# Second attention: the causal mask of a head added by sixteen 32x32 products instead of four 128x128 ones

## The chip, the cores and the metric

The kernel runs on one core of one Trainium2 chip. The metric is device microseconds from start to end of one execution; lower is better. A core has a matrix engine (PE), whose weight loads the profile shows apart (PEld), a vector engine (DVE), an activation engine (ACT), a general engine (POOL) and a queue that issues transfers (SP). PE writes its results to eight PSUM banks, which DVE and ACT read.

## What is computed

A transformer of four layers over x with 16 sequences of 256 tokens and 128 features. The layers are an attention with 2 heads, a feed-forward part, a second attention with 16 heads of 8 features and a causal mask, and the same feed-forward part again. The second attention is what matters here:

```python
qkv = encodings @ attn_w.T + attn_b
q, k, v = jnp.split(qkv, 3, axis=-1)          # 16 heads, 8 features each
mask = jnp.arange(n)[:, None] <= jnp.arange(n)[None, :]
scores = jnp.einsum('bhki,bhqi->bhkq', k, q) / math.sqrt(HEAD)
scores = jnp.where(mask, scores, NEG_INF)
probs = jax.nn.softmax(scores, axis=2)        # over the keys
combined = jnp.einsum('bhkq,bhkl->bhql', probs, v)
out = out @ out_w.T + out_b
```

## The kernel before

The 16 sequences are worked in 8 blocks of 2 sequences (512 tokens), block 0 to block 7, and each layer runs over the 8 blocks before the next layer begins, with some overlap at the seams. Every engine has its own program in a fixed order, written out by hand; semaphores tie them together. Blocks 1 to 6 run in a loop or in copies of its body.

In the second attention a block has 8 steps (n = 0 to 7), each for one group of 4 heads and one sequence. Scores are made twice. `pe_first` makes them queries by keys for the block after the current one, so that DVE (`dve_first`, two reductions b_segment_max at L1599) can take each query's maximum. `pe_second` makes them keys by queries for the current block, with the maximum already in the operands, and ACT (`act_exp`, b_prob at L1504) takes the exponential. POOL zeroes the masked part of the probabilities (L1709), and `pe_values` multiplies them with v.

The four heads of a group lie in four groups of 32 rows of the operands, `rows_of(j)`. A product over 32 rows occupies a quarter of the array's rows, so four heads' products can run side by side. In the trace they are the matmuls with shape 32*128 of f_h_lo and f_h_hi (these tiles hold q and k in this layer); head j writes PSUM bank j of first_pass. The values' products have shape 128*16: all rows, 16 columns of weights. The mask is added inside the same accumulation: for each head a product of the identity ident_b with the tile mask (0, or -1e30 above the diagonal), shape 128*128 with 256 moving columns, both bf16.

One step on PE is, in this order: pe_second for heads 0 and 1, pe_first with its mask products, pe_second for heads 2 and 3, pe_values of the step before, and in most steps a piece of other work (transposes, projections of a later block, the output projection). What PE waits for:

- pe_first waits for DVE's reductions of the step before, since there is one set of first_pass banks; in steps 0 and 4 also for the rows that a transfer brings.
- each pe_second waits for ACT's exponential of the pair before, since there is one pair of second_pass banks.
- pe_second's second half stands behind the mask products in PE's queue.

The firsts of block 0 are made earlier, one after each chunk of the last feed-forward block of the layer ahead (`pe_front`, block LAST = 7 there). I call this the front.

Transfers are issued by SP in order (`sp_out`, then `sp_rows`): the weighted values of the block before go to DRAM (b_o_dram), come back as oT and den, the inverse of den goes out and back, and only then are q and k of the block two ahead stored and loaded again in their row layout. `sp_out` begins when ACT has copied the last group's values in step 0.

The mask and the identity are made by POOL near the start of the program (`pool_b_constants`, L272 to L281). The first attention, which runs before that layer, has its own POOL work in each block: rstd (L207), X plus bias (L774), the rotated keys a_kT and queries a_qT (L766), and the low parts of weights, wlo (L851). DVE there waits for most of these, and scales a_prob (L666) and normalises xn (L182) from SBUF to SBUF.

In the last block of the second attention no firsts are made; two products of ident_b with 512 columns of mask per step fill PE there.

Of the kernel before, what the change touches and what calls it, by code (L numbers as in the profile page):

```python
# [18 lines left out]
BF16 = mybir.dt.bfloat16  # L19
# [66 lines left out]
def build(nc, io):  # L86
    ctx = ExitStack()
    with ctx:
# [166 lines left out]
        ident_b = sb("b_ident", [P, P], BF16)  # L255
        mask = sb("b_mask", [P, GROUPS, P], BF16)

# [13 lines left out]
        def pool_b_constants(pool):  # L271
            nc.gpsimd.memset(constant_rows[:, :, :], 0.0).then_inc(s_cr, 1)  # L272
            nc.gpsimd.memset(ident_b[:, :], 0.0).then_inc(s_cp, 1)
            nc.gpsimd.memset(mask[:, :, :], 0.0).then_inc(s_cp, 1)
            pool.wait_ge(s_cr, 1)
            nc.gpsimd.memset(constant_rows[0:1, 1, :], 1.0).then_inc(s_cr, 1)

            pool.wait_ge(s_cp, 2)
            nc.gpsimd.affine_select(out=ident_b[:, :], in_=ident_b[:, :], compare_op=ALU.not_equal, fill=1.0,
                                    base=0, pattern=[[-1, P]], channel_multiplier=1).then_inc(s_cp, 1)  # L280
            nc.gpsimd.affine_select(out=mask[:, 0:3:2, :], in_=mask[:, 0:3:2, :], compare_op=ALU.is_ge, fill=MASKED,  # L281
                                    base=0, pattern=[[0, 2], [-1, P]], channel_multiplier=1).then_inc(s_cp, 1)

# [9 lines left out]
        def attention_a(link):  # L293
# [475 lines left out]
            def pool_body(pool, b, before, one, two):  # L769
# [5 lines left out]
                if one:  # L775
                    pool_rope(pool, b.after(1), 1)
                if two and not is_block(b, 0):
                    ffn["beside"]["pool"](pool, b.after(2))
# [414 lines left out]
        def attention_b(link):  # L1193
# [97 lines left out]
            def pe_first(pe, m, n):  # L1291
# [7 lines left out]
                for qt, into in ((1, slice(P, 3 * P)), (0, slice(0, P))):  # L1299
                    for j in range(GROUPS):  # L1300
                        mm(first_pass[:, j, into], q[rows_of(j), g, at + qt * P:at + (qt + 1) * P],
                           k[rows_of(j), g, at:at + (qt + 1) * P], start=qt == 1, stop=False)
                for j in range(GROUPS):
                    out = first_pass[:, j, 0:3 * P].rearrange("p (c k) -> p c k", c=3)
                    last = mm(out[:, 0:3:2, :], ident_b[:, :], mask[:, 0:3:2, :], start=False, stop=True)
                last.then_inc(s_p1, 1)
# [65 lines left out]
            def pe_step(pe, b, n, before, one, two, parts=None):  # L1372
# [15 lines left out]
                if not one and n > 2:  # L1388
                    if n == 3:
                        pe.wait_ge(nxt["split_written"], 1)  # L1390
                    for _ in range(2):
                        mm(misc[:, :], ident_b[:, :], mask[:, :, :].rearrange("p g k -> p (g k)"))
                if n:
# [588 lines left out]
```

## Time and profile before

| | |
|---|---|
| runs of the kernel (us) | 740.25, 737.65, 735.57; median 737.65 |
| span of the profiled execution | 729.4 us |
| own time of the profiled execution | not recorded beside the span; the median lies 8.25 us above the span |
| instructions in the profile | 13978 |
| busy: PE / DVE / ACT / POOL | 665.8 / 497.1 / 451.8 / 425.8 us |
| mean granted clock of PE | 0.990 |
| first attention, feed-forward, front | 0 to 124, 124 to 303, 303 to 328 us |
| second attention, second feed-forward | 328 to about 545, then to the end |

The busy times say how much work an engine has, not who is waited for. The time is a chain of work from start to end; an instruction made shorter gives time back only where it lies on that chain, and only until something else is late.

### The profile page before, as it was taken

The page shows a single profiled execution, that of the slowest core. Times are in us where ns is not written, and L with a number is a line of the kernel's source. Part 1 is how long each engine was busy: PE and PEld are TensorE (multiplying, and loading weights), DVE is VectorE, ACT ScalarE, POOL GpSimd, SP SyncE. Part 2 cuts the span into 40 slices and gives each one's busy share as a digit, 9 for nine tenths or more (in the row PEclk, how much of TensorE's full clock was granted, in tenths as well). Part 3 has the DMA queues.
Part 4 walks back from the last instruction along what each step waited for, and adds up shares of the span by engine and source line. Part 5 has one row for each costly group of instructions (what it writes and reads, how often), then busy time and mean ns, then how long its engine had stood idle before and what let it go on. Part 6 is the DMA issues. An engine that isn't in the chain of part 4 may idle for free.

```text
span 729.4 us, 13978 instructions
## 1 busy us (share of the span) xinstructions
PE 665.8 (91%) x4716; PEld 467.1 (64%) x4716; DVE 497.1 (68%) x958; ACT 451.8 (62%) x801; POOL 425.8 (58%) x443
## 2 busy tenths in 40 slices
PE   3889997799999999998999999998988999999997
PEld 1455654478777776675555655655546777877785
DVE  6769998577656688456867867865668667776521
ACT  2668887456666666445666666665675566566664
POOL 4545543277877777434444554543565777777773
PEclk9989999999999999999999999999999999999999
DMA  6101230000000001730645754745122000000000
GB/s 191 40 21 41 57 37 1 1 1 1 1 0 0 1 0 45 245 116 29 229 144 184 260 165 169 249 148 182 38 69 92 0 15 15 14 0 15 16 14 30
DMA packets 33028, 52.47 MB, mean 72 GB/s; under 512 B 4560, under 2 KB 9680, under 8 KB 32976
## 3 DMA queue, kind: packets, MB, share of 16 engines
q1 hardware_dynamic: 32784, 51.53, 22.4%
q8 instruction: 30, 0.49, 0.3%
q10 hardware_dynamic: 192, 0.26, 0.1%
q14 instruction: 22, 0.18, 0.1%
HBM read 27.15 MB, written 24.38 MB: 71 GB/s over the span
## 4 chain that ended last, share of the span: by engine, by line
PE 57%; DVE 18%; issue 8%; ACT 7%; DMA 6%; POOL 2%; SPq 1%; DVEq 1%; ACTq 0%; POOLq 0%
PE banks L220 54%; DVE b_segment_max L1599 3%; ACT b_prob L1504 3%; DVE xn L182 3%; DMA b_o_dram<-b_o 3%; DVE a_mx L652 2%; DMA f_h_lo<-b_k_dram 1%; ACT a_prob L553 1%; DMA b_den<-b_o_dram 1%; DVE f_gate L1088 1%; DVE f_h_hi L1091 1%; PE banks L212 1%; PE banks L977 1%; DVE f_hidden L1094 1%; DVE a_prob L666 1%
## 5 line engine op out<-in xcount | busy, mean ns | idle before, releaser
L1158 POOL TENSOR_TENSOR f_g_lo<-f_gelu,f_g_hi 128x512 fp32r<-128x512 f32 x127 | 162.9, 1292 | 53.5 <-ACT f_g_hi L1044 53.0
L1043 ACT ACTIVATE f_gelu<-banks,cols 128x512 f32<-128x512 f32 x128 | 88.3, 690 | 130.6 <-PE banks L220 108.7
L1709 POOL TENSOR_SCALAR_AFFINE_SELECT b_prob<-b_prob 128x512 f32<-128x512 f32 x128 | 81.5, 638 | 107.0 <-ACT b_prob L1504 106.5
L1599 DVE TENSOR_REDUCE b_segment_max<-banks 128x6 f32<-128x768 f32 x128 | 116.1, 949 | 33.4 <-PE banks L220 33.2
L1504 ACT ACTIVATE b_prob<-banks 128x768 f32<-128x768 f32 x128 | 102.3, 806 | 55.7 <-PE banks L220 55.7
L220 PE MATMUL banks<-f_g_hi,whi 128*128 128x512 f32 x320 | 130.4, 408 | 1.9 <-POOL f_g_lo L1158 1.4
L220 PE MATMUL banks<-f_g_lo,whi 128*128 128x512 f32 x320 | 126.7, 396 | 0.0
L1151 POOL TENSOR_TENSOR f_h_lo<-f_hidden,f_h_hi 128x512 fp32r<-128x512 f32 x60 | 77.6, 1293 | 62.8 <-DVE f_hidden L1094 61.1
L220 PE MATMUL banks<-f_h_hi,whi 128*128 128x512 f32 x256 | 104.3, 407 | 6.1 <-POOL f_h_lo L1151 3.3
L220 PE MATMUL banks<-f_h_lo,whi 128*128 128x512 f32 x256 | 101.5, 396 | 0.0
L1044 ACT ACTIVATE f_g_hi<-banks,cols 128x512 fp32r<-128x512 f32 x128 | 87.4, 682 | 0.0
L1088 DVE SCALAR_TENSOR_TENSOR f_gate<-f_tanh,banks 128x512 f32<-128x512 f32 x64 | 43.3, 677 | 53.3 <-ACT f_tanh L1035 53.3
L220 PE MATMUL banks<-f_xn_split,whi 128*128 128x512 f32 x256 | 71.6, 402 | 1.3 <-DVE f_hidden L1094 1.3
L182 DVE TENSOR_SCALAR xn<-X,mv,rstd 128x128 f32<-128x128 f32 (+1 forms) x104 | 72.3, 760 | 0.4 <-POOL rstd L207 0.4
L220 PEld LDWEIGHTS banks<-f_g_hi,whi 128*128 128x128 f32 x320 | 60.3, 188 | 17.6 <-POOL f_g_lo L1158 3.5
L220 PEld LDWEIGHTS banks<-f_g_lo,whi 128*128 128x128 f32 x320 | 60.4, 189 | 13.2 <-issue 0.2
L220 PEld LDWEIGHTS banks<-f_h_hi,f_h_lo 32*128 32x128 f32 x512 | 37.0, 184 | 45.7 <-ACT b_prob L1504 23.6
L220 PE MATMUL banks<-f_h_hi,f_h_lo 32*128 32x128 f32 (+1 forms) x512 | 54.9, 300 | 10.8 <-ACT b_prob L1504 7.2
L220 PEld LDWEIGHTS banks<-f_h_hi,whi 128*128 128x128 f32 x256 | 48.2, 188 | 22.8 <-POOL f_h_lo L1151 4.4
L220 PE MATMUL banks<-b_prob,b_values 128*16 128x256 f32 (+1 forms) x1024 | 56.1, 332 | 2.2 <-POOL b_prob L1709 1.5
L220 PEld LDWEIGHTS banks<-f_xn_split,whi 128*128 128x128 f32 x256 | 48.1, 190 | 15.1 <-DVE f_hidden L1094 2.0
L220 PEld LDWEIGHTS banks<-f_h_lo,whi 128*128 128x128 f32 x256 | 48.2, 188 | 11.1 <-issue 0.5
(125 smaller groups left out, 1061.0 us busy)
## 6 DMA issues: line engine op xcount, KB each, us to landing
f_h_hi<-b_q_dram SPq DMA_DIRECT2D x16, 512.0 KB, 4.0
f_h_lo<-b_k_dram SPq DMA_DIRECT2D x16, 512.0 KB, 5.0
b_o_dram<-b_o SPq DMA_DIRECT2D x8, 1024.0 KB, 4.3
b_q_dram<-b_q_hi SPq DMA_DIRECT2D x16, 256.0 KB, 3.3
b_k_dram<-b_k_hi SPq DMA_DIRECT2D x16, 256.0 KB, 3.6
w_stage<-in_wF SPq DMA_DIRECT2D x8, 352.0 KB, 3.2
b_q_dram<-b_q_lo SPq DMA_DIRECT2D x8, 256.0 KB, 3.4
b_k_dram<-b_k_lo SPq DMA_DIRECT2D x8, 256.0 KB, 3.7
```

Of the source, the lines that this page charges most:

```text
L182: nc.vector.tensor_scalar(xn[:, s, :], X[:, bass.ds(TILES * t + s, 1), :], mv[:, s, 0:1], rstd[:, s:s + 1], ALU.subtract, ALU.mult).then_i ...
L212: last = nc.tensor.transpose(bank[:, s * P:(s + 1) * P], xn[:, s, :], ident[:, :])
L220: return nc.tensor.matmul(out, lhsT, rhs, start=start, stop=stop)
L652: nc.vector.reduce_max(mx[s][:, :, :], score[:, :, :].rearrange("p h (q k) -> p h q k", q=2), AX.X).then_inc(s_mx, 1)
L1043: nc.scalar.activation(gf[c % 2][:, :], z_bank[c % 2], ACT.Gelu, scale=scale).then_inc(s_gf, 1)
L1044: nc.scalar.activation(hi[:, c, :], z_bank[c % 2], ACT.Gelu, scale=scale).then_inc(s_ghi[c % 2], 1)
L1088: nc.vector.scalar_tensor_tensor(out=uu[slot][:, :], in0=th[slot][:, :], scalar=1.0, in1=a[:, :], op0=ALU.add, op1=ALU.mult).then_inc(s_u, 1)
L1151: nc.gpsimd.tensor_tensor(hlo[n.odd][:, c, :], hf[c % 2][:, :], hhi[n.odd][:, c, :].bitcast(F32), ALU.subtract).then_inc(s_hlo[c % 2], 1)
L1158: nc.gpsimd.tensor_tensor(lo[:, c, :], gf[c % 2][:, :], hi[:, c, :].bitcast(F32), ALU.subtract).then_inc(s_glo[c % 2], 1)
L1504: nc.scalar.activation(prob[n % 2][:, p, :, :, :], second_banks(b, p)[:, :, 0:3 * P].rearrange("p b (c q) -> p c b q", c=3), ACT.Exp, scal ...
L1599: nc.vector.reduce_max(seg[:, g, s, 2 * p:2 * p + 2, :], first_pass[:, 2 * p:2 * p + 2, 0:3 * P].rearrange("p b (c k) -> p b c k", c=3), A ...
L1709: nc.gpsimd.affine_select(out=pr, in_=pr, compare_op=ALU.is_ge, fill=0.0, base=0, pattern=[[0, 4], [1, P]], channel_multiplier=-1).then_in ...
```

## The change

For each head j and each group i of 32 queries, the mask is now added by a product of 32 rows (the identity's rows and columns of `rows_of(j)`, shape 32*32) with 256 moving columns from the mask's rows `rows_of(j)`. Four such products make up what was one, so a step has 16 mask products instead of 4. The products of one head use that head's row group only; the 16 products of a step name 16 different 32x32 parts of the array. For this the mask tile grows from 4 x 128 to 7 x 2 x 128 columns: one diagonal position for each difference of i and j. Its zeroing and its filling move on POOL from the start of the program into blocks 5 and 6 of the first attention, and are 1792 columns wide instead of 512 and 256. The fillers of the last block read the first 512 columns of the new tile.

```diff
-        mask = sb("b_mask", [P, GROUPS, P], BF16)
+        mask = sb("b_mask", [P, 2 * GROUPS - 1, 2, P], BF16)
...
-            nc.gpsimd.memset(mask[:, :, :], 0.0).then_inc(s_cp, 1)
...
-            nc.gpsimd.affine_select(out=mask[:, 0:3:2, :], in_=mask[:, 0:3:2, :], compare_op=ALU.is_ge, fill=MASKED,
-                                    base=0, pattern=[[0, 2], [-1, P]], channel_multiplier=1).then_inc(s_cp, 1)
+        def pool_mask_zero(pool):
+            nc.gpsimd.memset(mask[:, :, :, :], 0.0).then_inc(s_cp, 1)
+
+        def pool_mask_rows(pool):
...
+            pool.wait_ge(s_cp, 3)
+            nc.gpsimd.affine_select(out=mask[:, :, :, :], in_=mask[:, :, :, :], compare_op=ALU.is_ge, fill=MASKED,
+                                    base=-QUART * (GROUPS - 1), pattern=[[QUART, 2 * GROUPS - 1], [0, 2], [-1, P]],
+                                    channel_multiplier=1).then_inc(s_cp, 1)
...
                     pool_rope(pool, b.after(1), 1)
+                if is_block(b, LAST - 2):
+                    pool_mask_zero(pool)
+                if is_block(b, LAST - 1):
+                    pool_mask_rows(pool)
...
-                for j in range(GROUPS):
-                    out = first_pass[:, j, 0:3 * P].rearrange("p (c k) -> p c k", c=3)
-                    last = mm(out[:, 0:3:2, :], ident_b[:, :], mask[:, 0:3:2, :], start=False, stop=True)
+                for i in range(GROUPS):
+                    for j in range(GROUPS):
+                        out = first_pass[rows_of(i), j, 0:3 * P].rearrange("p (c k) -> p c k", c=3)
+                        last = mm(out[:, 0:3:2, :], ident_b[rows_of(j), rows_of(j)],
+                                  mask[rows_of(j), GROUPS - 1 + i - j, :, :], start=False, stop=True)
                 last.then_inc(s_p1, 1)
...
-                        mm(misc[:, :], ident_b[:, :], mask[:, :, :].rearrange("p g k -> p (g k)"))
+                        mm(misc[:, :], ident_b[:, :], mask[:, 0:2, :, :].rearrange("p g c k -> p (g c k)"))
```

POOL's order in blocks 5 and 6 of the first attention, before; f_h_lo, the next work of POOL, is the feed-forward layer's:

```order
L204 TENSOR_TENSOR veps<-mv,eps_t 128x4
L207 TENSOR_TENSOR rstd<-veps,mhalf 128x4
L774 TENSOR_TENSOR X<-X,rows 128x512
L766 TENSOR_TENSOR a_kT<-a_straight,a_turned 128x512
L851 TENSOR_TENSOR wlo<-w_stage,whi 128x704
L766 TENSOR_TENSOR a_qT<-a_straight,a_turned 128x512
L204 TENSOR_TENSOR veps<-mv,eps_t 128x4
L207 TENSOR_TENSOR rstd<-veps,mhalf 128x4
L774 TENSOR_TENSOR X<-X,rows 128x512
L766 TENSOR_TENSOR a_kT<-a_straight,a_turned 128x512
L798 TENSOR_TENSOR X<-X,rows 128x512
```

And now, with the two instructions on the mask behind a_kT of either block:

```order
L207 TENSOR_TENSOR rstd<-veps,mhalf 128x4
L782 TENSOR_TENSOR X<-X,rows 128x512
L774 TENSOR_TENSOR a_kT<-a_straight,a_turned 128x512
L282 MEMSET b_mask 128x1792
L863 TENSOR_TENSOR wlo<-w_stage,whi 128x704
L774 TENSOR_TENSOR a_qT<-a_straight,a_turned 128x512
L204 TENSOR_TENSOR veps<-mv,eps_t 128x4
L207 TENSOR_TENSOR rstd<-veps,mhalf 128x4
L782 TENSOR_TENSOR X<-X,rows 128x512
L774 TENSOR_TENSOR a_kT<-a_straight,a_turned 128x512
L288 AFFINE_SELECT b_mask<-b_mask 128x1792
L810 TENSOR_TENSOR X<-X,rows 128x512
```

The zeroing now stands ahead of wlo, and the filling ahead of the last X plus bias; both were ahead of everything in the layer before.

PE's order in one step of the second attention, before (b_ident and b_mask are the mask products, b_values with b_prob the values):

```order
L220 MATMUL banks<-f_h_hi,f_h_lo 128x128 x2
L220 MATMUL banks<-f_h_lo,f_h_hi 128x256 x4
L220 MATMUL banks<-f_h_lo,f_h_hi 128x128 x4
L220 MATMUL banks<-b_mask,b_ident 128x2x128 x4
L220 MATMUL banks<-f_h_hi,f_h_lo 128x2x128 x2
```

And now:

```order
L220 MATMUL banks<-f_h_hi,f_h_lo 128x128 x2
L220 MATMUL banks<-f_h_lo,f_h_hi 128x256 x4
L220 MATMUL banks<-f_h_lo,f_h_hi 128x128 x4
L220 MATMUL banks<-b_mask,b_ident 32x2x128 x16
L220 MATMUL banks<-f_h_hi,f_h_lo 128x2x128 x2
```

Nothing has changed its place on PE; 4 products over 128 rows have become 16 over 32 rows.

## Rows read from the trace of the kernel before

**Rows 1.** The page: busy times by engine, and the chain that ended last.

```profile
PE 665.8 (91%) x4716; PEld 467.1 (64%) x4716; DVE 497.1 (68%) x958; ACT 451.8 (62%) x801; POOL 425.8 (58%) x443
PE 57%; DVE 18%; issue 8%; ACT 7%; DMA 6%; POOL 2%; SPq 1%; DVEq 1%; ACTq 0%; POOLq 0%
```

**Rows 2.** Groups by form: busy us, mean ns of one, idle before them.

```profile
L220 PE MATMUL banks<-b_prob,b_values 128*16 128x256 f32 x512 | 41.8, 388 | 2.2 <-POOL b_prob L1709 1.5 <-ACT b_o L1512 0.7
L220 PE MATMUL banks<-b_mask,b_ident 128*128 128x256 bf16 x256 | 39.5, 277 | 0.0
```

**Rows 3.** Timeline, step 2 of a middle block: start, length, engine, what, [idle, releaser].

```profile
420.00 0.81 ACT L1504 ACTIVATE b_prob<-banks 128x768 f32<-128x768 f32 x1
...
420.45 0.61 PE L220 MATMUL banks<-b_mask,b_ident 128*128 128x256 bf16 x4
420.99 0.44 PE L220 MATMUL banks<-f_h_hi,f_h_lo 32*128 32x256 f32 x4
421.10 1.82 DVE L1599 TENSOR_REDUCE b_segment_max<-banks 128x6 f32<-128x768 f32 x2 [1.08 <-PE banks L220]
...
421.21 0.22 PE L220 MATMUL banks<-f_h_hi,f_h_lo 32*128 32x128 f32 x2
421.36 0.41 PE L220 MATMUL banks<-b_prob,b_values 128*16 128x256 f32 x4
```

**Rows 4.** Timeline, step 7 of the same block.

```profile
437.99 0.81 ACT L1504 ACTIVATE b_prob<-banks 128x768 f32<-128x768 f32 x1 [0.84 <-PE banks L220]
438.11 0.61 PE L220 MATMUL banks<-b_mask,b_ident 128*128 128x256 bf16 x4
438.86 0.29 PEld L220 LDWEIGHTS banks<-f_h_hi,f_h_lo 32*128 32x128 f32 x4 [0.42 <-ACT b_prob L1504]
```

**Rows 5.** The chain in the front, two pieces: start, length, what.

```profile
306.54 1.00 PE banks L220 x12
...
312.36 4.74 PE banks L220 x28
```

**Rows 6.** The chain: two waits for loaded rows, at the start of blocks 2 and 6.

```profile
381.14 4.99 DMA f_h_lo<-b_k_dram
...
490.48 5.78 DMA f_h_lo<-b_k_dram
```

**Rows 7.** The chain in blocks 5 and 6 of the first attention.

```profile
102.42 2.12 DVE a_prob L666 x2
...
115.36 1.82 DVE xn L182 x3
```

**Rows 8.** Timeline of POOL and DVE in the same two blocks.

```profile
102.43 1.69 POOL L851 TENSOR_TENSOR wlo<-w_stage,whi 128x704 fp32r<-128x704 f32 x1
...
109.89 0.58 DVE L666 TENSOR_SCALAR a_prob<-a_prob,a_inv 128x256 f32<-128x256 f32 x2
...
115.31 1.27 POOL L798 TENSOR_TENSOR X<-X,rows 128x512 f32<-128x512 f32 x1
...
115.36 1.30 DVE L182 TENSOR_SCALAR xn<-X,mv,rstd 128x128 f32<-128x128 f32 x1
```

**Rows 9.** Timeline of POOL at the start of the program.

```profile
7.95 0.34 POOL L273 MEMSET b_ident<- 128x128 bf16 x1
8.24 0.62 POOL L274 MEMSET b_mask<- 128x512 bf16 x1
...
9.38 0.28 POOL L279 TENSOR_SCALAR_AFFINE_SELECT b_ident<-b_ident 128x128 bf16<-128x128 bf16 x1
9.62 0.40 POOL L281 TENSOR_SCALAR_AFFINE_SELECT b_mask<-b_mask 128x256 bf16<-128x256 bf16 x1
```

**Rows 10.** Windows: stretch, length, busy time (count) of PE, PEld, DVE, ACT, POOL, clock, DMA.

```profile
412.80:440.30 27.50, 25.41 (x321) 15.69 (x321) 21.17 (x38) 17.86 (x25) 13.78 (x20) 1.00 0.58 194
```

More of the change, by code:

```diff
@@ L273, in pool_b_constants @@
             nc.gpsimd.memset(ident_b[:, :], 0.0).then_inc(s_cp, 1)
-            nc.gpsimd.memset(mask[:, :, :], 0.0).then_inc(s_cp, 1)
             pool.wait_ge(s_cr, 1)
             nc.gpsimd.memset(constant_rows[0:1, 1, :], 1.0).then_inc(s_cr, 1)
-            pool.wait_ge(s_cp, 2)
+            pool.wait_ge(s_cp, 1)
             nc.gpsimd.affine_select(out=ident_b[:, :], in_=ident_b[:, :], compare_op=ALU.not_equal, fill=1.0,
                                     base=0, pattern=[[-1, P]], channel_multiplier=1).then_inc(s_cp, 1)
-            nc.gpsimd.affine_select(out=mask[:, 0:3:2, :], in_=mask[:, 0:3:2, :], compare_op=ALU.is_ge, fill=MASKED,
-                                    base=0, pattern=[[0, 2], [-1, P]], channel_multiplier=1).then_inc(s_cp, 1)
+        def pool_mask_zero(pool):
[5 more added lines that the diff above has]
+                                    channel_multiplier=1).then_inc(s_cp, 1)
         def sp_b_constants(sp):
```

## The prediction

> **What bounds the kernel now.** I read the page first, then the chain that ended last, then the timelines of single steps. The page gives PE 91% busy and more than half of the chain [rows 1]. That invites the conclusion that any microsecond taken from PE is won. The busy time of matmuls overlaps their own pipeline, so it can't decide this, and the steps have to be read one by one. The mask products are 256 in number and 39.5 us busy [rows 2], in 64 steps: 8 in the front, 56 in blocks 0 to 6 of the second attention.
>
> Step 2 of a middle block [rows 3] is one in which PE ends last. The exponential ends at 420.81, and a pe_second released by ACT starts about 0.05 after that in other steps. The next pe_second starts only at 420.99, behind the mask products. So PE is late by 0.13. Step 7 [rows 4] is of the other kind: the last mask product starts at 438.11 + 0.61 - 0.27 = 438.45, the exponential ends at 438.80, and the load for the next pe_second starts at 438.86 after 0.42 us of idleness put down to ACT. There PE is early. In the blocks I read, steps 1 and 2 are of the first kind and steps 0 and 3 to 7 of the second: their exponential starts late, since ACT does another piece first or since PE's side work ahead of them was long. That side work is not touched.
>
> In the front the chain alternates between PE's firsts (a piece of 12 matmuls, 1.00 us) and DVE's two reductions, or stays on PE for a whole chunk [rows 5]. Twice the chain of the second attention goes through the transfers of SP's round [rows 6], at the starts of blocks 2 and 6, and once more in block 6 behind the denominators. In the first attention the chain runs along DVE, and two of its pieces are instructions that DVE does from SBUF to SBUF while POOL is at work [rows 7, 8].
>
> **What a mask costs, before and after.** Before: the four products start 0.11 apart ((0.61 - 0.27) / 3), the last starts 0.34 after the first, and the next pe_second 0.54 after it (420.45 to 420.99). DVE starts 0.65 after it (421.10) [rows 3]. After: no row shows a 32*32 product. The nearest are those that already share the array. Four values' products, which take a quarter of the columns each, start within 0.02 of each other (a row of four lasts 0.41, one of them 0.39) [rows 2, 3]; the two 32-row products of a pe_second do so too (a row of two lasts 0.22) [rows 3]. If all 16 parts run side by side at that pace, the last starts 15 x 0.007 = 0.10 after the first. The change of shape behind it costs 0.15 after a product over 32 rows (last one at 421.21, values at 421.36) and 0.20 after one over 128 rows (420.79 to 420.99), so the next pe_second could start at 0.25 instead of 0.54: 0.29 less. DVE, by the 0.22 that a product over 32 rows with the same stream lasts, at 0.10 + 0.22 + 0.04 = 0.36 instead of 0.65: again 0.29 less. The other bound is that the four column groups of one head take turns, at 0.11 each: then the last starts at 0.34 as before and about 0.05 is left to gain. I take 0.29, since both kinds of sharing are in the trace, the column kind with a wide operand (f32) too.
>
> Of tiling the Trainium skill (TensorEngine Tiling (Array Packing), Key Properties) says that a change of tiling mode, unlike a change of tile, drains the engine. That speaks against the change in the front, where the mask products had the shape of the feed-forward products behind them and now have not. The rows agree that shapes cost: 0.15 to 0.20 us at each switch [rows 3]. I count it by rows: before, the feed-forward products followed in the same shape, and could stream when the last mask product had, at 0.34 + 0.11 = 0.45; now a switch lies between, and they can at 0.10 + 0.15 = 0.25. So 0.20 is left of 0.29 where PE goes on with the feed-forward part.
>
> **The front: -1.8 us.** Eight masks. In step 0 DVE is still at the low part of k when the mask is done: 0. After steps 1, 2, 4 and 7 the chain goes over to DVE: 4 x 0.29 = 1.16. After steps 3, 5 and 6 it stays on PE (pieces of 4.7 us) [rows 5]: 3 x 0.20 = 0.60. Sum 1.8.
>
> **Second attention: -0.9 us.** Per block, steps 1 and 2 give what ACT leaves, 0.13 to 0.2 each, together 0.3; DVE's reductions, which end late ahead of the firsts in these steps, come earlier by 0.29 and don't stand in the way. Steps 0 and 3 to 7 give nothing. SP's round starts in step 0, before these gains. Where the rows it loads come last (at the ends of blocks 1 and 5), or the denominators do (block 6), the 0.3 of that block is given back in a longer wait for a transfer [rows 6]. In block 2 both steps follow such a wait and are ACT's. What stays is 0.3 each in blocks 0, 3 and 4: 0.9. In blocks 3 and 4 the chain passes through no transfer.
>
> **First attention: +2.7 us.** The cost of zeroing: 128 columns take 0.34, 512 take 0.62, so 0.72 ns for one more column, and 1792 take 1.55. Filling: 0.28 for 128, 0.40 for 256, so 1.83 for 1792 [rows 9]. POOL, 58% busy, has idle time for both. But POOL's time is not what counts. Two a_prob instructions take 0.58 us when POOL is idle, and 2.12 when wlo runs; the one xn instruction started beside X plus bias takes 1.30, until POOL is done [rows 7, 8]. So such a DVE instruction stands still until POOL's current one ends. The Trainium skill says the same (SBUF — State Buffer, SBUF: two separate sides): the pair of ports is an exclusive lock, and the loser blocks fully; the trace agrees.
>
> In block 5 zeroing starts where wlo did (102.43), and wlo follows at 103.9 until 105.7. The first a_prob then waits for the zeroing's end, the second for wlo's: done at about 105.7 instead of 104.54, +1.2. In block 6 the second xn waits for the end of the filling (117.14), the third for X plus bias (118.4), the fourth follows: 118.7 instead of 117.2, +1.5. DVE is on the chain at both places [rows 7] and has no gap to take this up until the layer ends. The lower bound: where DVE slips through between two POOL instructions, block 5 costs nothing and block 6 about 0.5. I take 2.7, since the pair X plus bias behind a_kT shows a waiting instruction at each. At the start of the program POOL saves 1.0 us (0.62 and 0.40) [rows 9]; PE's first projections cover that, 0.
>
> **The sum.** -1.8 - 0.9 + 2.7 = 0.0. The page gives only a span for the profiled execution, 729.4; the median is 8.25 above it, and I leave that difference alone. Forecast: 737.6 us. About 1% (7.4 us) is what I take a measurement of this kernel to tell from no change.
>
> **Rivals.**
> (a) POOL's work is mostly hidden: only 0.5 is lost, 737.65 - 2.7 + 0.5 = 735.4. For it: POOL is 42% idle. Against: rows 8. Chance 0.13.
> (b) The column groups of a head take turns: the gain shrinks to 2.7 x 0.05 / 0.29 = 0.5, and the time is 739.9. For it: nothing in the trace has both kinds of sharing at once. Chance 0.09. By the Trainium skill (TensorE: Matmul & The Clock Gate, Measured speedup vs the span model) sixteen such tiles overlap with about 4 ns for each; as an estimate from that page the last would start at 0.06 instead of 0.10, and the sum would be 0.4 us lower. No row here shows it.
> (c) PE is the bound in every step after all: 64 x 0.29 = 18.6 won, 721.8. For it: 91% busy and 57% of the chain. Against: the idle time for ACT in rows 4, in six of eight steps. Chance 0.03.
> (d) Slower: PE can't begin its instructions fast enough. A block has 321 recorded matmuls in 27.5 us [rows 10], one in 0.086; with 12 x 8 = 96 more in each block it is 417, and the block keeps its time only if PE begins one every 0.066. If the pace were limited to 0.070, a block would take 29.2, +1.7, and seven blocks +12: about 750. Against: the values' products begin within nanoseconds of each other, but they may have been queued during a wait, so that says nothing about a lasting pace. It decides from 0.066 on. Chance 0.09. By the Trainium skill (TensorE: Matmul & The Clock Gate, Step-by-step) decoding in software costs about 62 ns per matmul; as an estimate 417 x 0.062 = 25.9, just below the block. No run here shows that figure.
>
> **How the numbers follow.** Forecast 0.66, (a) 0.13, (b) 0.09, (c) 0.03, (d) 0.09. The first three lie between 735 and 740. The transfers that the chain waits for differ by 0.8 us among themselves [rows 6], and the runs of before spread over 4.7 us. So the range is 733.0 to 742.0, which leaves out (c) and (d). Faster by over 1%: (c) and a little, 0.04. Slower by over 1%: (d) and a little, 0.10. Within 1%: 0.86.
>
> **What the profile will show.** 1024 mask products of shape 32*32, in each step 16 within 0.1 us of each other, and pe_second or the reductions 0.25 and 0.36 behind the first. Steps 1 and 2 released by ACT. The firsts in the front earlier, 8 of them together by 1.8 us. A block of the second attention still 27 us and more long; longer waits for the loaded rows. In the first attention zeroing of about 1.55 and filling of about 1.8 us, with an a_prob and two xn standing still beside them. Wrong would make me: mask products a tenth of a microsecond apart (b), idle time of PE between them with no releaser (d), or blocks shorter by a microsecond or more (c).

## The result and the profile after

The changed kernel takes 750.49 us (748.99 to 755.17, 4 runs) where the kernel before, timed beside it, takes 736.93 (735.57 to 740.25). The ratio is 1.0225, interval 1.0175 to 1.0275: slower by some 13.6 us, where 737.6 was forecast. The profiled execution has a span of 748.7 us and a time of its own of 750.4. In every run for which both are known the time is 1.7 to 1.85 us above the span, and not 8.25, so the execution profiled before, with a span of 729.4, took some 731.2 us by estimate and was one of the fast ones of its kernel. The two traces are therefore 19.3 us apart where the medians are 13.6 apart, and the stretches compared below add up to the larger figure.

The page after, to be laid beside [rows 1]: busy times, PE's granted clock in 40 slices (tenths of full speed), instruction queue, chain.

```profile
PE 670.3 (90%) x5481; PEld 466.8 (62%) x5484; DVE 502.6 (67%) x958; ACT 453.9 (61%) x801; POOL 429.1 (57%) x443
PEclk9999998999999999996997889996799999999999
q8 instruction: 44, 0.72, 0.4%
PE 57%; DVE 14%; DMA 8%; ACT 8%; issue 7%; SPq 2%; POOL 2%; DVEq 0%; ACTq 0%; POOLq 0%
```

The clock row is the news. Before it read as follows, with an instruction queue of 30 packets:

```profile
PEclk9989999999999999999999999999999999999999
q8 instruction: 30, 0.49, 0.3%
```

PE's busy time has gone up by 4.5 us although 256 products of 128 rows became 1024 of 32 that share the array. The windows view, cut where the first exponential of each block of the second attention starts (first attention, feed-forward, front, then blocks 0 to 6), shows where. Columns: stretch, length, busy PE, PEld, DVE, ACT, POOL with instructions, granted clock, DMA share, GB/s. After:

```profile
0.00:131.30 131.30, 104.06 (x590) 62.09 (x590) 108.04 (x261) 88.70 (x244) 62.83 (x68) 0.97 0.22 54
131.30:305.50 174.20, 166.50 (x738) 129.49 (x736) 115.54 (x215) 103.65 (x168) 121.21 (x104) 0.99 0.06 21
305.50:330.70 25.20, 22.94 (x273) 16.27 (x276) 16.47 (x21) 12.11 (x19) 10.20 (x8) 1.00 0.45 152
330.70:365.40 34.70, 30.93 (x412) 18.04 (x411) 20.63 (x37) 18.00 (x25) 11.31 (x19) 0.75 0.25 79
365.40:392.60 27.20, 23.24 (x416) 14.09 (x408) 20.87 (x38) 17.88 (x25) 14.00 (x21) 1.00 0.58 196
392.60:427.80 35.20, 27.15 (x424) 16.73 (x424) 22.50 (x47) 18.15 (x26) 13.99 (x21) 0.80 0.56 185
427.80:457.80 30.00, 26.60 (x422) 16.07 (x418) 20.00 (x28) 18.08 (x25) 13.66 (x20) 0.84 0.46 147
457.80:485.40 27.60, 23.22 (x415) 14.10 (x409) 21.27 (x38) 17.81 (x25) 13.75 (x21) 1.00 0.59 196
485.40:512.60 27.20, 23.31 (x417) 14.42 (x416) 21.01 (x38) 17.84 (x26) 13.91 (x21) 1.00 0.59 198
512.60:543.90 31.30, 28.52 (x416) 17.74 (x420) 19.48 (x35) 16.39 (x23) 13.88 (x21) 0.66 0.26 87
```

Before, the same stretches (front, block 0, block 2, block 6; the blocks between them are 27.3 to 27.6 long):

```profile
303.10:329.30 26.20, 24.11 (x173) 17.57 (x172) 16.12 (x20) 12.17 (x20) 10.22 (x8) 1.00 0.43 149
329.30:358.50 29.20, 26.06 (x312) 16.23 (x312) 20.36 (x37) 17.80 (x25) 11.27 (x19) 1.00 0.31 95
...
386.00:413.40 27.40, 25.54 (x324) 15.79 (x328) 20.48 (x38) 17.78 (x25) 13.69 (x21) 1.00 0.59 196
...
495.80:524.70 28.90, 24.64 (x320) 15.62 (x324) 19.11 (x34) 16.11 (x22) 13.89 (x21) 0.94 0.27 94
```

The front is 1.0 shorter. Blocks 1, 4 and 5, at a clock of 1.00, are as long as before to 0.4. Block 0 is longer by 5.5, block 2 by 7.8, block 3 by 2.5, block 6 by 2.4, and these are the four with a clock under 1.00. Since a stretch is granted either 2.4 GHz or 1.2 GHz (an entry of 1.00 or 0.50), a block's time at 1.2 GHz is its length times twice what its clock lacks of 1: 17, 14, 10 and 21 us. The first attention and the feed-forward layer together account for 2.4 more.

What 1.2 GHz does to a step is to be read in PE's timeline of block 0 (start, length, engine, what):

```profile
343.73 1.48 PE L220 MATMUL banks<-b_prob,b_values 128*16 128x256 f32 x16
345.14 2.08 PE L220 MATMUL banks<-xnT,wB 128*128 128x512 f32 x2
...
354.46 0.84 PE L220 MATMUL banks<-b_prob,b_values 128*16 128x256 f32 x16
```

The values of a step take 1.48 us at 1.2 GHz and 0.84 at 2.4. From 338.6 to 352.2 PE is busy 13.4 of 13.6 us and waits for nobody: it is the bound there. In the same steps before, at a clock of 1.00, it was busy 12.5 of 13.6.

Block 2 holds a second thing, in the chain that ended last (start, length, what):

```profile
422.38 0.82 ACT b_prob L1518
423.20 3.78 issue
426.98 0.70 PE banks L220 x4
```

The exponential ends at 423.20 and PE's next product starts 3.78 us later, with nothing that the profile shows it to wait for. This is the place where PE's program jumps back to the start of its loop over two blocks (it does so once, between blocks 2 and 3). The clock falls to 1.2 GHz during the stand, at about 423.9, and stays there until 437.6, so block 3's time at 1.2 GHz is the rest of this stretch:

```profile
420.50:423.90 3.40, 2.19 (x50) 1.32 (x48) 2.87 (x4) 1.62 (x2) 1.19 (x2) 1.00 0.70 240
423.90:427.30 3.40, 0.32 (x4) 0.33 (x6) 1.36 (x10) 0.00 (x0) 0.09 (x1) 0.50 0.84 278
```

The other 10 us at 1.2 GHz in block 2, from 393.2 to 403.4, lie ahead of the stand and begin while PE waits 1.19 us for the loaded rows. Before, no such stand is in the chain.

### The profile page after: what moved, and what is told of

Same layout as the page of the kernel before. It is cut to its first block, busy times and chain, and to the rows that moved or that the text cites. A ratio compares the mean times of both kernels' runs of the same rounds, so it can differ in the third digit from the quotient of the medians.

```text
span 748.7 us, 15511 instructions
## 1 busy us (share of the span) xinstructions
PE 670.3 (90%) x5481; PEld 466.8 (62%) x5484; DVE 502.6 (67%) x958; ACT 453.9 (61%) x801; POOL 429.1 (57%) x443
## 4 chain that ended last, share of the span: by engine, by line
PE 57%; DVE 14%; DMA 8%; ACT 8%; issue 7%; SPq 2%; POOL 2%; DVEq 0%; ACTq 0%; POOLq 0%
PE banks L220 54%; ACT b_prob L1518 4%; DMA b_o_dram<-b_o 3%; DVE xn L182 2%; DMA f_h_lo<-b_k_dram 2%; DVE a_mx L660 2%; DMA b_k_dram<-b_k_lo 2%; SPq L1791 1%; PE banks L212 1%; ACT a_prob L561 1%; DMA b_den<-b_o_dram 1%; DVE a_prob L674 1%; DVE f_gate L1100 1%; DVE f_h_hi L1103 1%; PE banks L989 1%
## 5 line engine op out<-in xcount | busy, mean ns | idle before, releaser
L220 PE MATMUL banks<-f_g_hi,whi 128*128 128x512 f32 x320 | 131.0, 409 | 1.9 <-POOL f_g_lo L1170 1.4
L220 PE MATMUL banks<-f_g_lo,whi 128*128 128x512 f32 x320 | 127.3, 398 | 0.0
L220 PE MATMUL banks<-f_h_hi,whi 128*128 128x512 f32 x256 | 104.7, 409 | 6.1 <-POOL f_h_lo L1163 3.4
L220 PE MATMUL banks<-f_h_lo,whi 128*128 128x512 f32 x256 | 101.7, 397 | 0.0
L220 PE MATMUL banks<-f_h_hi,f_h_lo 32*128 32x256 f32 (+1 forms) x512 | 60.7, 329 | 26.2 <-ACT b_prob L1518 19.9
L220 PEld LDWEIGHTS banks<-f_h_hi,f_h_lo 32*128 32x128 f32 x512 | 41.8, 208 | 61.2 <-ACT b_prob L1518 31.6
L220 PE MATMUL banks<-f_xn_split,whi 128*128 128x512 f32 x256 | 71.8, 403 | 1.3 <-DVE f_hidden L1106 1.3
L220 PEld LDWEIGHTS banks<-f_g_hi,whi 128*128 128x128 f32 x320 | 60.5, 189 | 17.8 <-POOL f_g_lo L1170 3.1
L220 PEld LDWEIGHTS banks<-f_g_lo,whi 128*128 128x128 f32 x320 | 60.7, 190 | 13.3 <-issue 0.2
L220 PE MATMUL banks<-b_prob,b_values 128*16 128x256 f32 (+1 forms) x1024 | 63.5, 368 | 1.4 <-POOL b_prob L1723 1.3
L220 PEld LDWEIGHTS banks<-f_h_hi,whi 128*128 128x128 f32 x256 | 48.3, 189 | 23.4 <-POOL f_h_lo L1163 4.4
L220 PEld LDWEIGHTS banks<-f_xn_split,whi 128*128 128x128 f32 x256 | 48.2, 191 | 14.8 <-DVE f_hidden L1106 2.0
L220 PEld LDWEIGHTS banks<-f_h_lo,whi 128*128 128x128 f32 x256 | 48.3, 189 | 11.1 <-issue 0.5
```

The lines of the kernel that those rows point to most:

```text
L220: return nc.tensor.matmul(out, lhsT, rhs, start=start, stop=stop)
```

## The experiments

All ratios are to the kernel before, timed on the same chip beside them: 732.9 us for the first four, 733.1 for the next four, 732.8 for the last four (medians). Theory A: PE has less work between its waits, so its clock falls. Theory B: the longer instruction stream costs time where PE jumps. C: POOL's share.

**POOL's part alone** (e1_pool_only): four whole products as before, read from the large tile.

```diff
-                for i in range(GROUPS):
...
+                for j in range(GROUPS):
+                    out = first_pass[:, j, 0:3 * P].rearrange("p (c k) -> p c k", c=3)
+                    last = mm(out[:, 0:3:2, :], ident_b[:, :], mask[:, GROUPS - 1, :, :], start=False, stop=True)
```

> The changed kernel with its four 128x128 mask products put back (reading the diagonal position of the large mask tile); what is left of the change is the place and size of POOL's two mask instructions. Theory A (the granted clock of PE falls because the small products leave PE less active) and theory B (the longer instruction stream of PE costs a refill at the loop's jump and elsewhere) both expect the clock as before, 0.99, and only POOL's price: 736.9 + 2.5 = 739.4. Theory C (POOL's move costs most of the 13 us) expects about 750.

Measured 737.08 (734.39 to 740.73, 10 runs), ratio 1.0056 (1.0035 to 1.0077): +4.1 us. No stand at the jump, and one stretch of 3.4 us at 1.2 GHz in block 0. C is real and small, though more than the 2.5 us expected.

**PE's part alone** (e2_pe_only): small products, the large tile built at the start of the program.

```diff
-                if is_block(b, LAST - 2):
-                    pool_mask_zero(pool)
-                if is_block(b, LAST - 1):
-                    pool_mask_rows(pool)
```

What is taken out here stands in the program's first instructions on POOL.

> The changed kernel with the large mask tile built at the start of the program, where the old one was; the sixteen small products stay. Theories A and B expect most of the loss to stay: 750.5 - 2.5 + up to 1 for the longer POOL work at the start = 748 to 749, with stretches at half clock in the second attention. Theory C expects about 737.

Measured 752.61 (742.96 to 755.54, 4 runs), ratio 1.0275 (1.0235 to 1.0316). The stand is there (3.96 us of "issue" at 414.89). The four runs are 742.96, 750.42, 754.8 and 755.54, and even the first is 10 us above the kernel before. The loss is PE's.

**Small products and whole ones that add zero** (e3_small_and_zero).

```diff
+                for j in range(GROUPS):
+                    out = first_pass[:, j, 0:3 * P].rearrange("p (c k) -> p c k", c=3)
+                    last = mm(out[:, 0:3:2, :], ident_b[:, :], mask[:, 2 * GROUPS - 1, :, :], start=False, stop=True)
```

> The changed kernel with four 128x128 products of 256 columns more in each step, which add an all-zero part of the mask tile: more work for PE than in either kernel, and a still longer instruction stream. Theory A expects the half-clock stretches of the second attention to shrink to about those of the kernel before, and a time between 738 and 745, faster than the changed kernel although it does more. Theory B expects the stall at the loop's jump to stay or grow and the time at 750 or above.

Measured 748.99 (746.8 to 753.79), ratio 1.0227. The granted clock is back at 0.98 for the span, but the added products stand between the scores and DVE's reduction in every step, and the stand at the jump is there (3.36 us at 422.48). The total lies between the two forecasts (738 to 745, and 750 or above) and says nothing by itself. The clock row does: it has one slice under 9 in the second attention's part (slices 18 to 30) where the changed kernel has six.

```profile
PEclk9989999899999999999999899999999999999999
```

**No mask products at all** (e4_no_mask): the scores of later keys stay in.

```diff
-                for j in range(GROUPS):
-                    out = first_pass[:, j, 0:3 * P].rearrange("p (c k) -> p c k", c=3)
-                    last = mm(out[:, 0:3:2, :], ident_b[:, :], mask[:, 0:3:2, :], start=False, stop=True)
```

> The kernel before with the mask products left out of the first scores (the maxima are then taken over masked scores too): less work for PE and a shorter instruction stream. Theory A expects PE's clock to fall at least as often as in the changed kernel and a time of 745 or more, slower than the kernel before although it does less. Theory B expects no stall at the jump, a clock of 0.99, and 732 to 736.

Measured 752.92 (739.93 to 755.29, 4 runs): by the medians 20 us more than the kernel before, with 256 products less. The runs are wide apart, 739.93, 751.25, 754.58 and 755.29, at mean clocks of 0.949, 0.930, 0.924 and 0.923. The fastest is still 7 us above the median of the kernel before and slower than all 13 of its runs (up to 736.01). The windows of blocks 0 to 4, from the run of 751.25:

```profile
327.10:364.30 37.20, 31.88 (x276) 18.94 (x274) 21.41 (x46) 18.09 (x27) 11.56 (x19) 0.64 0.25 78
364.30:396.10 31.80, 26.02 (x292) 15.45 (x290) 20.19 (x31) 18.09 (x25) 13.65 (x20) 0.78 0.50 166
396.10:423.10 27.00, 21.14 (x286) 12.96 (x280) 21.26 (x38) 17.81 (x26) 13.79 (x21) 1.00 0.59 200
423.10:456.90 33.80, 27.46 (x296) 16.26 (x296) 21.07 (x38) 18.07 (x26) 13.89 (x21) 0.75 0.48 157
456.90:483.90 27.00, 21.10 (x293) 13.20 (x288) 21.35 (x41) 17.83 (x26) 13.77 (x21) 1.00 0.59 198
```

There is no stand at a jump and no longer instruction stream here (29 packets), so B has no part in it. The row also gives the most that any mask could ever have saved: a block at 2.4 GHz without a mask is 27.0 us long, 0.4 under before.

**The loop written out** (e5_unrolled): the changed kernel, PE's six middle blocks one after the other.

```diff
-                run_inner(pe, pe_body)
+                for t in range(1, BLOCKS - 1):
+                    pe_body(pe, Block(t // 2, t % 2), True, True, t < BLOCKS - 2)
```

> The changed kernel with PE's six middle blocks of the second attention written out one after the other in place of the loop over two blocks; data, order and instructions of every block are the same. In the changed kernel PE stands 3.78 us without a wait at the jump back of that loop, and the granted clock is at 1.2 GHz for part of the block behind it. Theory B (the longer instruction stream costs time where PE jumps) expects the stand to be gone and with it the cold stretch of the block behind it: about -4 to -9 us against the changed kernel, some 742 to 746 us. Theory A (PE has less to do between its products, and the clock falls for that) expects the other cold stretches of the second attention, some 45 us in the changed kernel, to stay in number: about 745 to 750 us. No change at all (750 us) would say that the stand is only another form of waiting for instructions that unrolled code pays too.

Measured 742.3 (733.95 to 745.58, 4 runs), ratio 1.0146 (1.0116 to 1.0176). By the ratios (1.0146 and 1.0225) that is some 6 us under the changed kernel, and the two intervals just touch. The stand is gone, though PE's code still takes 41 packets of instructions against 44, so it hung on the jump and not on their number alone. What is left varies with the clock from run to run: 733.95 at a mean of 0.981, 743.64 at 0.957.

**Small products in the front alone** (e6_front_only), the mask as one row of 320 columns read at a shifting offset and built at the start:

```diff
+        def mask_at(rows, d):
+            at = P - QUART * (1 + d)
+            return mask[rows, at:at + P].unsqueeze(1).to_broadcast([rows.stop - rows.start, 2, P])
...
+                            last = mm(out[:, 0:3:2, :], ident_b[rows_of(j), rows_of(j)], mask_at(rows_of(j), i - j),
+                                      start=False, stop=True)
```

> The kernel before with the 32-row mask products in the front alone (the four steps of block 0 between the first feed-forward part and the loop), and the whole products of 128 columns in every block behind it. The mask is one row of 320 columns that is read at a shifting offset, so it is built at the start by one fill and one selection of about the cost of before, and nothing of it lies on POOL later. The front has 48 instructions per head round more than before, in straight code. Theory A expects the clock of blocks 1 to 7 as before (about 0.99 for the span) and, if the front stays at 2.4 GHz, a front that is 0.9 to 1.8 us shorter: 731 to 733 us beside 733 for before. If the front's own gain makes the block behind it cold, as in the changed kernel, 736 to 741 us. Theory B alone (instructions at the jump) expects no stand at the jump back and -1 us. POOL's part (C) is absent here: its a_prob and xn rows should be as before.

Measured 733.04 (730.45 to 740.81, 12 runs), ratio 1.0016 (0.9987 to 1.0044). The clock of the second attention holds, and no gain is to be seen in the total.

**As many products, but as long a stream** (e7_row_mode): 16 products of 32 rows over all 128 columns.

```diff
+                        at = P - QUART * (1 + i - j)
+                        last = mm(out[:, 0:3:2, :], ident_w[rows_of(j), at:at + P], mask_at(rows_of(j), i - j),
+                                  start=False, stop=i == GROUPS - 1)
```

> The kernel before with 16 mask products in place of 4, but each of 32 rows over all 128 columns (32*128 tiles): product i of head j writes all 128 queries with the mask of queries 32i to 32i+31 and zero for the others, so the number of instructions is that of the changed kernel, while each row group streams 4 x 256 columns in turn, as long as the four whole products of before. The mask and the shifted unit matrix are built at the start at about the old cost. Theory A in the form that the time in which PE streams holds the clock: cold stretches of the second attention near zero, while the stand at the loop's jump back is there (3 to 4 us): 736 to 741 us. Theory A in the form that the share of the array at work counts: cold stretches as in the changed kernel (some 60 us), 747 to 753 us. Theory B alone: the jump's 3 to 4 us and what the block behind it loses to the clock, 738 to 743 us.

Measured 741.57 (740.15 to 745.06), ratio 1.0115 (1.0089 to 1.014), with a stand of 4.60 us at the jump. That is what theory B alone expected (738 to 743), and just above the form of theory A that counts the time in which PE streams (736 to 741). The mean clocks of the four runs are 0.975 to 0.981, where the changed kernel's are 0.936 to 0.958. A step's 16 products last 0.82 us from the first one's start to the last one's end (439.93 to 440.75), beside 0.33 for the small ones and 0.61 for the four whole ones:

```profile
439.93 0.39 PE L220 MATMUL banks<-b_mask,b_ident 32*128 32x256 bf16 x4
440.08 0.22 PE L220 MATMUL banks<-f_h_lo,f_h_hi 32*128 32x128 f32 x2
440.14 0.61 PE L220 MATMUL banks<-b_mask,b_ident 32*128 32x256 bf16 x12
```

**Its loop written out** (e11_rows_unrolled), with the edit of e5_unrolled.

> The kernel with 16 mask products of 32 rows over 128 columns, and PE's six middle blocks written out without the loop. The stand at the jump (4.6 us in the looped one) and what the block behind it lost to the clock should be gone: theory A with B expects 741.6 less some 6 us, 734 to 737 us, near the kernel before, with few cold stretches. If 16 instructions in place of 4 cost the clock or the fetch of instructions by themselves, it stays at 739 to 742.

Measured 735.7 (732.68 to 738.39, 10 runs), ratio 1.0045 (1.0019 to 1.007), as expected. Its interval lies clear under that of e7_row_mode: the jump costs some 5 us there. Sixteen mask instructions a step cost some 3 us (1.4 to 5.1 by the interval) when they stream at least as long as the four and PE doesn't jump.

**One product more in the same mode** (e8_first_twice):

```diff
+                for j in range(GROUPS):
+                    mm(first_pass[:, j, P:3 * P], q[rows_of(j), g, at + P:at + 2 * P], k[rows_of(j), g, at:at + 2 * P])
```

> The changed kernel with the four scores products of the second query half made twice (the first of the two is overwritten by the second), 32 rows x 128 columns x 256 columns each: PE gets back some 0.2 us of work in every step, in the row-group mode that it is in already, and four instructions more. Theory A expects the cold stretches of the second attention to shrink from some 62 us to below 20 and the time to fall to 741 to 746 us, although the kernel does more work; theory B expects no gain: the jump's stand stays, the steps are 0.1 to 0.2 us longer, 750 to 756 us.

Measured 745.82 (741.1 to 748.6), ratio 1.0192 (1.0162 to 1.0222). It lies at the upper end of theory A's forecast (741 to 746), the stand is there (3.82 us), the mean clocks of the four runs are 0.959 to 0.977, and its interval overlaps that of the changed kernel. It leans to A and decides nothing.

**Small products, loop written out, mask built at the start** (e9_small_unrolled): the edits of e5 and the mask of e6.

> The small products everywhere, with two of the suspected costs taken out at once: PE's six middle blocks written out without the loop, and the mask as one row of 320 columns read at a shifting offset, built at the start at the old cost, so that nothing of it is on POOL later. What is left is PE's shorter work alone. If the parts add up: the unrolled kernel's ratio 1.0146 less POOL's 0.0056 is 1.009, some 739 to 740 us beside 733, with cold stretches of the second attention as in the unrolled kernel (15 to 45 us, different from run to run) and the first attention as in the kernel before. If PE's shorter work is worth what the steps show at 2.4 GHz (0.3 us in each block, 0.9 in the front) and the clock holds: 730 to 731 us.

Measured 741.3 (738.65 to 742.23), ratio 1.0106 (1.0059 to 1.0153), clocks of the four runs 0.954 to 0.970. PE's shorter work alone costs some 8 us, at clocks that lie below the 0.98 to 0.99 of most runs of the kernel before. With POOL's 0.0056 it makes 0.0162, beside the 0.0146 of e5_unrolled. This kernel and e11_rows_unrolled have the same number of instructions, no jump and no mask work late on POOL, and differ in the work of the mask products, which stream longer there and over all 128 columns. All four runs here (738.65 and more) are above all ten there (738.39 and less). So it is PE's shorter work and not the number of instructions that costs the time.

**The idle time filled** (e10_idle_filled): e9 and, in blocks 1 to 6,

```diff
+                if one and before:
+                    g, s = group((n - 1) % STEPS)
+                    if s == 0:
+                        wait(pe, s_oc, GROUPS * b.t + g)
+                    for _ in range(GROUPS):
+                        mm(o_bank[:, T:T + GROUPS * P - MASK_COLS], ident_b[:, :], mask[:, MASK_COLS:])
```

> The kernel of the label e9_small_unrolled, and in blocks 1 to 6 four whole products of the unit matrix with a zero part of the mask (192 columns each) into the half of the output bank that is free, behind the small mask products, where PE waits 0.3 to 0.8 us for the exponentials anyway. They are about 0.33 us of work that nobody waits for. Theory A (less PE work lets the clock fall) expects the clock of the second attention to hold and the gain of the small products to show at last: 729 to 732 us, 0 to 4 below before. If the fill delays the second scores where the wait is shorter than 0.33 us, the steps give back 0.1 each: 733 to 736. If the clock falls all the same, as in e9: 738 to 741.

Measured 737.53 (735.59 to 752.94, 12 runs), ratio 1.0067 (1.0034 to 1.0101). That is some 4 us under e9_small_unrolled with more work, though the two intervals overlap. It is above the 729 to 732 that theory A expected and above the 733 to 736 for a fill that delays the second scores, and it is not the version that beats the kernel before.

**No mask, idle time filled** (e12_no_mask_filled): the kernel of e4_no_mask (scores of later keys stay in), and in blocks 1 to 6 four whole products of 256 columns where e10 has its four.

> The kernel before without its mask products (the scores of later keys stay in, so the output differs), and in blocks 1 to 6 the same four whole products of 256 columns put back as work that nobody waits for: a zero part of the mask into the free half of the output bank, behind the first scores. Without the fill this kernel was at 752.9 us, 20 above before, with 71 us cold, although it does less. Theory A expects the clock of blocks 1 to 6 to come back and the time to fall under the kernel before: 725 to 731 us. If the loss without a mask had another cause than PE's activity, the fill changes nothing: 745 to 755 us.

Measured 734.48 (730.94 to 741.5, 10 runs), ratio 1.0029 (0.9991 to 1.0068): by the medians 18 us under the same kernel without the fill, of whose four runs three are above all ten here. The windows of blocks 0 to 3:

```profile
326.30:363.30 37.00, 31.70 (x274) 18.70 (x274) 21.30 (x46) 18.03 (x25) 11.50 (x19) 0.64 0.25 80
363.30:391.90 28.60, 26.76 (x320) 16.11 (x322) 20.08 (x32) 17.94 (x26) 13.71 (x20) 0.93 0.55 182
391.90:419.20 27.30, 25.55 (x328) 15.81 (x328) 21.22 (x38) 17.80 (x26) 13.75 (x21) 1.00 0.60 197
419.20:446.40 27.20, 25.19 (x326) 15.67 (x320) 20.92 (x38) 17.88 (x26) 13.97 (x21) 1.00 0.58 197
```

This pair shows A most clearly. Block 0, which has no fill, is the same in both kernels (37.0 and 37.2 us, clock 0.64). From block 1 on, the fill holds the clock, and blocks 1 and 3 fall from 31.8 and 33.8 to 28.6 and 27.2, though each holds 32 products more. The total missed the 725 to 731 expected. Block 0, which I had left unfilled, is 7.8 us longer than in the kernel before, which would account for it; that a fill there gives this back is not shown.

## Why the prediction was wrong

The forecast failed at the pricing in "Second attention: -0.9 us". It took PE's shorter work to be worth either a gain or nothing, at the clock of the rows it was read from. The row of a block showed 1.00 [rows 10], and I didn't ask whether it would stay there when PE does less. The runs showed in its place blocks with 10 to 21 us at 1.2 GHz, and, with the stand at the jump, 17.8 us lost in this term where 0.9 were to be won. "Steps 0 and 3 to 7 give nothing" was true of the wait for ACT and false of the clock: in these steps the 0.29 us saved became idle time of PE. The stand at the jump is missing from the forecast altogether. The Trainium skill (TensorE: Matmul & The Clock Gate, Part 1: The HAM clock gate) says that the slow clock is the default and activity releases it. These runs agree: with 256 products less the mean clock of e4_no_mask is 0.923 to 0.949, and with 192 put back (e12_no_mask_filled) 0.954 to 0.978. Point by point:

- **What a mask costs.** Right for PE, a little off for DVE. A step of block 4 after, at 2.4 GHz:

```profile
464.80 0.33 PE L220 MATMUL banks<-b_mask,b_ident 32*32 32x256 bf16 x16
465.06 0.29 PEld L220 LDWEIGHTS banks<-f_h_hi,f_h_lo 32*128 32x128 f32 x4
...
465.24 1.82 DVE L1613 TENSOR_REDUCE b_segment_max<-banks 128x6 f32<-128x768 f32 x2 [0.87 <-PE banks L220]
```

  The 16 start within 0.05 us (0.33 less the 0.278 of one); 0.10 was estimated from the values' products [rows 2, 3]. The next load is 0.26 behind the first product (0.25 forecast), DVE 0.44 (0.36 forecast). PE gains 0.28 a step, DVE 0.21. The sharing of rows and columns works, so rival (b) falls. By the Trainium skill (TensorE: Matmul & The Clock Gate, Measured speedup vs the span model) sixteen tiles cost about 4 ns each on top; the trace agrees, with 0.05 us for 15.
- **The front: -1.8.** The front is 1.0 shorter. The steps behind a wait for DVE are 2.70 us apart instead of 2.91, DVE's 0.21. Then the chain goes over to PE for good, where before it alternated [rows 5]:

```profile
307.08 1.74 DVE b_segment_max L1613 x2
308.82 0.04 issue
308.87 10.04 PE banks L220 x104
318.91 0.44 PE banks L989 x4
```

  What is late next was PE itself, with its feed-forward products: the term should have been limited by PE's own work in the stage.
- **Second attention: -0.9.** Measured +17.8 to the start of the last block: blocks 1, 4 and 5 change by 0.4 or less, blocks 0, 2, 3 and 6 are together 18.2 longer. Of block 2's 7.8, 3.78 are the stand at the jump, and block 3's 2.5 lie in the cold stretch (time at 1.2 GHz) that began in it; the other 14.4 of the 18.2 fall in the blocks that hold 62 us at 1.2 GHz. Between runs of one kernel the time goes with the clock in the same way: e4_no_mask took 739.93 us at a mean clock of 0.949 and 755.29 at 0.923, e5_unrolled 733.95 at 0.981 and 743.64 at 0.957. Even the small gain "in blocks 3 and 4" had no room. In block 4 after, the chain of waits is one round of transfers from end to end, of which these are the largest pieces:

```profile
460.61 5.07 DMA b_o_dram<-b_o
...
466.30 3.05 DMA b_den<-b_o_dram
...
475.65 4.79 DMA b_k_dram<-b_k_lo
...
480.95 4.90 DMA f_h_lo<-b_k_dram
```

  The round starts behind the first step's output and ends in the rows that the next block loads. PE's L220 has 3% of the chain of this stretch, where it had 52% in the same block before. So the round of transfers is what is late next in a block, and it comes soon: even without any mask a block is 27.0 us long (e4_no_mask).
- **First attention: +2.7.** Right in kind and nearly in size. POOL's two instructions (1.60 and 1.80 us, forecast 1.55 and 1.83) and the DVE instructions that stand beside them, to be laid beside [rows 7, 8]:

```profile
101.05 1.60 POOL L282 MEMSET b_mask<- 128x1792 bf16 x1
101.05 3.41 DVE L674 TENSOR_SCALAR a_prob<-a_prob,a_inv 128x256 f32<-128x256 f32 x2
102.60 1.72 POOL L863 TENSOR_TENSOR wlo<-w_stage,whi 128x704 fp32r<-128x704 f32 x1
...
114.67 3.94 DVE L182 TENSOR_SCALAR xn<-X,mv,rstd 128x128 f32<-128x128 f32 x4
115.24 1.80 POOL L288 TENSOR_SCALAR_AFFINE_SELECT b_mask<-b_mask 128x1792 bf16<-128x1792 bf16 x1
117.01 1.26 POOL L810 TENSOR_TENSOR X<-X,rows 128x512 f32<-128x512 f32 x1
```

  The pair a_prob takes 3.41 instead of 2.12, and the four xn end at 118.61, where 118.7 was forecast. The stages up to the front are 2.4 longer in this trace, and POOL's part alone measured +4.1 (+2.6 to +5.6 by its interval). Where the rest of it lies is open: there is one stretch at 1.2 GHz in its block 0, but what that cost isn't shown.
- **Rival (d)** had the time, 750, and not the cause. Blocks of some 417 products at 2.4 GHz keep 27.2 us, one product in 0.065, so PE does begin them fast enough. What the longer stream costs is a stand at one jump. That PE waits there for instructions to be fetched fits the packets (44 against 30) and is not shown.

What each cause is worth, from the ratios: POOL's part 0.0056, the jump 0.0079 (1.0225 less 1.0146, its cold stretch included), PE's shorter work 0.0106 (e9_small_unrolled). The sum, 0.0241, stands beside 0.0225 measured, but the split isn't firm. The jump is worth 0.0169 between the kernels without late mask work on POOL (e2_pe_only less e9_small_unrolled) and 0.0070 with the 32*128 products (e7_row_mode less e11_rows_unrolled), and POOL's part doesn't show at all between the changed kernel and e2_pe_only (1.0225 and 1.0275). That each of the three costs something is shown; their sizes differ by up to 7 us from pair to pair. Open is also how much of the 0.0079 is the stand itself (3.78 us are 0.0051) and how much the clock behind it, since the clock differs between runs of one kernel; and whether a fill in block 0 too would bring the gain that e6_front_only and e10_idle_filled don't show. I know of no version that beats the kernel before.

## What to carry to other kernels

Work of PE that seems to be hidden behind a wait may be what keeps its clock up: before making it shorter, ask not only who waits for it but what the granted clock does when the saved time becomes idle time, and read the clock row of the result first. Where a saving lands in a stage that a round of transfers or the engine's own other work closes right behind, it has no upside to set against that. An edit that multiplies instructions inside a loop can also cost time at the jump back: look there for "issue" in the chain.

## What the runs showed of the chip

- Removing 256 matmuls made the kernel 20 us slower by the medians (7 to 22 by the single runs), and putting 192 back that nobody waits for made it 18 us faster (e4_no_mask, e12_no_mask_filled).
- In blocks at 1.00, PE was busy 25.5 of 27.4 us before, 23.2 of 27.2 with small products and 21.1 of 27.0 without a mask. So blocks with less work of PE can stay at 2.4 GHz too; what decides in which of them the clock falls is open. In e4_no_mask it fell five times between 330 and 545 us, and PE was never idle for more than 1.75 us at a time there.
- At its loop's one jump back PE stood 3.4 to 4.6 us in all five kernels with 16 or more mask products a step inside the loop, and the clock fell to 1.2 GHz during each of these stands. There was no stand in the kernels with four or none there, nor in straight code with 16.
- Sixteen 32*32 products of 256 columns start within 0.05 us of each other and are done in 0.33, a quarter of the array's rows and columns each.
